# Layer 0's source sums: one burst of matmuls a quad, or four rounds spread over the next quad's blocks

## The reference

```python
def _L0_gnn_ref(x, edge_index, pos, gate_w1, gate_w2, msg_w1, msg_w2):
    row, col = (edge_index[0], edge_index[1])
    e = jnp.concatenate([x[row], x[col]], axis=-1)                        # 206250 x 128
    g1 = _lrelu(jnp.einsum('ef,hgf->heg', e, gate_w1))                    # 4 heads x 64
    alpha = _lrelu(jnp.einsum('heg,hog->heo', g1, gate_w2))               # 4 heads x 1
    a = pos[col][None, :, None] * jnp.exp(alpha)
    seg = lambda t: jax.ops.segment_sum(t, row, num_segments=N_NODES)
    rowsum = jax.vmap(seg)(a)
    inv = 1.0 / rowsum + 1e-16
    alpha_n = a * inv[:, row]
    m1 = _lrelu(jnp.einsum('ef,hgf->heg', e, msg_w1))                     # 4 heads x 128
    beta = _lrelu(jnp.einsum('heg,hog->heo', m1, msg_w2))                 # 4 heads x 64
    out_h = jax.vmap(seg)(alpha_n * beta)
    return jnp.mean(out_h, axis=0)
```

## Time and profile before

| | |
|---|---|
| median of 3 runs | 6655.64 us (6654.76 to 6658.46) |
| the profiled execution's own time | 6656.1 us, its span 6654.2 us |
| TensorE matmul, busy | 4382.8 us, 66% |
| VectorE, busy | 4799.1 us, 72% |
| GpSimd, busy | 3779.0 us, 57% |
| ScalarE, busy | 2634.2 us, 40% |
| layer 0's loop over blocks, about 700 to 4200 us | TensorE busy in 930.6 of 1000 us, VectorE in 836.3, ScalarE in 688.9 |
| TensorE's granted clock in that stretch | 1.00 of 2.4 GHz |

### The profile page before, as it was taken

How to read it: one execution, slowest core, us unless ns; L and a number is a source line. 1 busy time by engine, 2 the same in 40 slices (tenths; PEclk the granted TensorE clock), 3 DMA queues, 4 the chain that set the end, 5 groups by cost and what they waited for, 6 DMA issues and landing times.

```text
span 6654.2 us, 117791 instructions
## 1 busy us (share of the span) xinstructions
PE 4382.8 (66%) x24069; PEld 2598.3 (39%) x24069; DVE 4799.1 (72%) x10127; ACT 2634.2 (40%) x6054; POOL 3779.0 (57%) x3799
## 2 busy tenths in 40 slices
PE   3611999999999999999999999233333333333334
PEld 1211444444444444444444444133333333333333
DVE  6986788888888888888888888755555555555554
ACT  1200666666666666666666666200000000000000
POOL 0100555555555555555555555177777777777774
PEclk9955999999999999999999999655555555555555
DMA  8301333333333333333333333222222222222222
GB/s 237 152 0 33 73 72 72 72 72 72 72 72 72 72 72 72 72 72 72 71 71 72 72 71 72 70 51 50 51 50 51 51 50 51 50 51 51 50 51 59
DMA packets 485530, 452.11 MB, mean 68 GB/s; under 512 B 281672, under 2 KB 372041, under 8 KB 483593
## 3 DMA queue, kind: packets, MB, share of 16 engines
q0 software_dynamic: 137360, 180.87, 16.9%
q1 hardware_dynamic: 321118, 246.02, 13.3%
q10 hardware_dynamic: 27008, 24.74, 1.5%
HBM read 363.66 MB, written 87.55 MB: 68 GB/s over the span
## 4 chain that ended last, share of the span: by engine, by line
PE 27%; DVE 26%; issue 20%; POOL 19%; DMA 3%; ACT 3%; POOLq 1%; DVEq 1%; SPq 0%; ACTq 0%
POOL ends L749 11%; POOL work L749 8%; PE ps_beta L1620 6%; DVE work L1158 6%; PE ps_beta L1628 5%; PE ps_hidden L1568 5%; DVE work L1287 5%; PE ps_hidden L1569 4%; DVE beta L1163 4%; DVE ends_hot L1147 3%; PE ps_sum L1639 3%; DVE terms L1179 2%; ACT scaled L813 2%; DVE parts L1179 2%; PE ps_T L1557 1%
## 5 line engine op out<-in xcount | busy, mean ns | idle before, releaser
L1767 PE MATMUL ps_beta<-work,equal 128*128 128x128 f32 x3232 | 834.1, 440 | 1548.5 <-DVE work L1492 1548.5
L652 POOL DMA_INDIRECT ends<-split_table,src_sb x808 | 775.7, 960 | 1456.0 <-issue 1429.7
L1767 PEld LDWEIGHTS ps_beta<-work,equal 128*128 128x128 f32 x3232 | 719.4, 328 | 1663.4 <-issue 1523.3
L1158 DVE TENSOR_TENSOR work<-work,ps_hidden 128x512 f32<-128x512 f32 x1616 | 1099.7, 680 | 256.6 <-ACT work L813 256.0
L1568 PE MATMUL ps_hidden<-ends_parts,w_high 128*128 128x512 f32 x2424 | 1109.4, 458 | 1.2 <-ACT ends_hot L860 1.2
L813 ACT ACTIVATE work<-ps_hidden 128x512 f32<-128x512 f32 x1616 | 965.0, 597 | 325.1 <-DVE work L1158 316.0
L652 POOL DMA_INDIRECT ends<-split_table,gather_sb x808 | 805.5, 997 | 502.4 <-issue 374.6
L749 POOL DMA_INDIRECT work<-src_table,src_sb x808 | 814.8, 1008 | 336.6 <-issue 239.2
L749 POOL DMA_INDIRECT ends<-src_table,gather_sb x808 | 863.5, 1069 | 245.6 <-issue 245.3
L1620 PE MATMUL ps_beta<-work,msg_w_sb 128*64 128x512 f32 x3232 | 871.6, 617 | 192.8 <-DVE work L1158 192.8
L1569 PE MATMUL ps_hidden<-ends_hot,window 128*128 128x512 f32 x2424 | 958.9, 396 | 0.0
(11 more groups left out here) (156 smaller groups left out, 6189.6 us busy)
## 6 DMA issues: line engine op xcount, KB each, us to landing
window<-window_table SPq DMA_DIRECT2D x808, 96.2 KB
dst_rows_sb<-by_src SPq DMA_DIRECT2D x404, 128.0 KB
window_table<-parts SPq DMA_DIRECT2D x50, 770.0 KB, 3.3
ends<-in_edge_attr SPq DMA_DIRECT2D x202, 128.0 KB
key_rows<-in_edge_attr SPq DMA_DIRECT2D x202, 128.0 KB
sums<-key_rows POOLq DMA_DIRECT2D x404, 32.6 KB
sums<-parts ACTq DMA_DIRECT2D x10, 1305.0 KB, 14.9
ends<-split_table,src_sb POOLq DMA_INDIRECT x808
```

Of the source, the lines that this page charges most:

```text
L652: pool.indirect_dma_start(out=ends[m][:, t, :], out_offset=None, in_=split_table, in_offset=bass.IndirectOffsetOnAxis(ap=src_windows[m][:, ...
L1158: nc.vector.tensor_tensor(hidden[k][:, :], scaled[k % NL][:, :], ps_hidden[k % NL][:, :], ALU.max).then_inc(hidden_ready, 1)
L1767: last = nc.tensor.matmul(ps_beta[0][0:WIN, 0:W1], hot[m % 2][:, t, :].bitcast(F32), terms1_windows[m][:, t, :], start=(m == 0 and t == 0) ...
```

## The change

`sum_quad` becomes `sum_round`: one tile t of all four blocks, 4 of the 16 matmuls. Round t = m is issued in block m of the next quad, at the place where the whole burst stood in block 0. The sum of a quad is then complete at the end of block 3 of the next one, so the terms and one-hot matrices are doubled (the second sets lie in `parts0` and in `equal1`), VectorE waits for `summed` of one quad further back, `copy_quad` comes in block 0 instead of block 1 and one quad later, and the adds come one quad later. Because the buffers alternate by quad, TensorE's and VectorE's loops turn once in two quads (`quads`); ScalarE's and GpSimd's still turn once a quad (`fours_late`, whose first two quads are written out). VectorE sets the ones of the second set of terms ahead of its loop.

```diff
+        def quads(eng, body):
+
+            for quad in range(3):
+                for m in range(4):
+                    body(4 * quad + m, quad, m, quad % 2)
+            with eng.Fori(1, (NQ - 3) // 2) as i:
+                for odd in (1, 0):
+                    for m in range(4):
+                        body(8 * i + 8 - 4 * odd + m, 2 * i + 2 - odd, m, odd)
+            for quad in range(NQ - 2, NQ):
+                for m in range(4):
+                    body(4 * quad + m, quad, m, quad % 2)
...
# GpSimd
-                adds = m >= 2 and not first_four(b)
+                adds = m >= 2 and not first_two(quad)
...
                 if adds:
-                    add_rows(quad - 1, 2 * m - 4)
+                    add_rows(quad - 2, 2 * m - 4)
...
# ScalarE
                 scale_chunk(b, 2)
-                if m == 1 and not first_four(b):
-                    copy_quad(quad - 1)
+                if m == 0 and not first_two(quad):
+                    copy_quad(quad - 2)
                 scale_chunk(b, 3)
...
                 scale_pair(NB - 1, 1)
+                copy_quad(NQ - 2)
                 copy_quad(NQ - 1)
...
# VectorE
-            def spread_weights(b, quad, m):
+            def spread_weights(b, quad, m, odd):
 
                 dve.wait_ge(exp_ready, b + 1)
                 if m == 0:
-                    wait(dve, summed, quad)
+                    wait(dve, summed, quad - 1)
...
+                for m in range(4):
+                    nc.vector.memset(terms_quads[1][m][:, :, W0 - 1:W0], 1.0).then_inc(ones_set, 1)
...
# TensorE
-            def sum_quad(b, quad):
-
-                pe.wait_ge(terms_ready, 2 * b + 2)
-                pe.wait_ge(src_hot_ready, b + 1)
-                wait(pe, quad_copied, quad)
-                for t in range(T):
-                    for m in range(4):
-                        last = nc.tensor.matmul(ps_sum[m * WIN0:(m + 1) * WIN0, 0:W0], hot_quad[m][:, t, :].bitcast(F32),
-                                                terms_quad[m][:, t, :], start=(t == 0), stop=(t == T - 1))
-                last.then_inc(summed, 1)
+            def sum_round(b, quad, t, odd):
+
+                if t == 0:
+                    pe.wait_ge(terms_ready, 2 * b + 2)
+                    pe.wait_ge(src_hot_ready, b + 1)
+                    wait(pe, quad_copied, quad)
+                for m in range(4):
+                    last = nc.tensor.matmul(ps_sum[m * WIN0:(m + 1) * WIN0, 0:W0], hot_quads[odd][m][:, t, :].bitcast(F32),
+                                            terms_quads[odd][m][:, t, :], start=(t == 0), stop=(t == T - 1))
+                if t == T - 1:
+                    last.then_inc(summed, 1)
...
                 pair_product(b, 1)
-                if m == 0 and begun:
-                    sum_quad(b - 1, quad - 1)
+                if not first_four(b):
+                    sum_round(b - 1 - m, quad - 1, m, 1 - odd)
```

More of the change, by code:

```diff
@@ L70 @@
 assert P * RUN >= EP and RUN == 4 * B and NP <= 1 << FIELD
-assert COPIES == 2 and NT % CH == 0 and NB >= 12 and ROWS * W0 % (P * 5) == 0
+assert NQ % 2 == 1 and COPIES == 2 and NT % CH == 0 and NB >= 12 and ROWS * W0 % (P * 5) == 0
 def gnn(nc, x, src, dst, src_rows, dst_rows, dst_all, edge_attr, edge_weight, node_vec, node_vec1, node_vec1_n2,
@@ L315, in gnn @@
         quad_copied = sem("quad_copied")
+        ones_set = sem("ones_set")
         gates_done = sem("gates_done")
@@ L348, in fours, with fours_late, first_two @@
                 body(NB - 4 + m, NB // 4 - 1, m)
+        def quads(eng, body):
[9 more added lines that the diff above has]
+                    body(4 * quad + m, quad, m, quad % 2)
+        def fours_late(eng, body):
+            for b in range(8):
+                body(b, b // 4, b % 4)
+            with eng.Fori(2, NQ - 1) as i:
+                for m in range(4):
+                    body(4 * i + m, i, m)
+            for m in range(4):
+                body(NB - 4 + m, NQ - 1, m)
         def early(b):
             return isinstance(b, int) and b < 2
+        def first_two(quad):
+            return isinstance(quad, int) and quad < 2
         def first_four(b):
@@ L677, in edges0_windows @@
                 if adds:
-                    add_rows(quad - 1, 2 * m - 3)
+                    add_rows(quad - 2, 2 * m - 3)
             pool.wait_ge(tail_step, 2)
@@ L693, in _ @@
                 pool.wait_ge(zeroed, 16 * 5 * COPIES)
-                fours(pool, edges0_windows)
-                for m in range(4):
-                    add_rows(NQ - 1, m)
+                fours_late(pool, edges0_windows)
+                for quad in range(NQ - 2, NQ):
+                    for m in range(4):
+                        add_rows(quad, m)
                 pool.wait_ge(quad_added, 64 * NQ)
@@ L1179, in weigh_pair, with match_src, edges0_windows @@
                 nc.vector.tensor_tensor(
-                    terms_quad[m][:, :, a * 2 * D:(a + 1) * 2 * D].rearrange("p t (h d) -> p t h d", d=D),
+                    terms_quads[odd][m][:, :, a * 2 * D:(a + 1) * 2 * D].rearrange("p t (h d) -> p t h d", d=D),
                     ps_beta[a][:, :].rearrange("p (t h d) -> p t h d", t=T, d=D),
-                    terms_quad[m][:, :, H * D + 2 * a:H * D + 2 * a + 2].unsqueeze(3).broadcast_to([P, T, 2, D]),
+                    terms_quads[odd][m][:, :, H * D + 2 * a:H * D + 2 * a + 2].unsqueeze(3).broadcast_to([P, T, 2, D]),
                     ALU.mult).then_inc(terms_ready, 1)
-            def match_src(b, quad, m):
+            def match_src(b, quad, m, odd):
                 if m == 0:
-                    wait(dve, summed, quad)
-                nc.vector.tensor_tensor(hot_quad[m], columns[:, 0:WIN0].unsqueeze(1).broadcast_to([P, T, WIN0]),
+                    wait(dve, summed, quad - 1)
+                nc.vector.tensor_tensor(hot_quads[odd][m], columns[:, 0:WIN0].unsqueeze(1).broadcast_to([P, T, WIN0]),
                                         src_offset[:, bass.ds(b * T, T)].unsqueeze(2).broadcast_to([P, T, WIN0]),
                                         ALU.is_equal).then_inc(src_hot_ready, 1)
-            def edges0_windows(b, quad, m):
+            def edges0_windows(b, quad, m, odd):
                 half, j = 2 * quad + m // 2, m % 2
@@ L1196, in edges0_windows @@
                 before_quad, before_m = quad - (m == 0), (m + 3) % 4
+                before_odd = 1 - odd if m == 0 else odd
                 if begun:
@@ L1378, in _ @@
             with dve.If(fit):
+                dve.wait_ge(row_out[0], 16 * ((NT + 1) // 2))
+                dve.wait_ge(row_out[1], 16 * (NT // 2))
+                dve.wait_ge(tables_split, 32)
+                for m in range(4):
+                    nc.vector.memset(terms_quads[1][m][:, :, W0 - 1:W0], 1.0).then_inc(ones_set, 1)
                 match_near(0, 0, 0)
@@ L1381, in _ @@
                 rectify_chunk_windows(0, 1)
-                fours(dve, edges0_windows)
+                quads(dve, edges0_windows)
                 rectify_pair(NB - 1, 1)
-                spread_weights(NB - 1, NQ - 1, 3)
-                match_src(NB - 1, NQ - 1, 3)
-                weigh_pair(NB - 1, 0, 3)
-                weigh_pair(NB - 1, 1, 3)
+                spread_weights(NB - 1, NQ - 1, 3, 0)
+                match_src(NB - 1, NQ - 1, 3, 0)
+                weigh_pair(NB - 1, 0, 3, 0)
+                weigh_pair(NB - 1, 1, 3, 0)
             with dve.Else():
@@ L1735, in _ @@
                 first_product_windows(0, 1, 0, 0)
-                fours(pe, edges0_windows)
+                pe.wait_ge(ones_set, 4)
+                quads(pe, edges0_windows)
                 turn_pair(NB - 1, 1)
-                sum_quad(NB - 1, NQ - 1)
+                for t in range(T):
+                    sum_round(NB - 1, NQ - 1, t, 0)
             with pe.Else():
```

27 lines of the change are left out of this document (13 added, 14 removed).

## The result

The changed kernel takes 6746.26 us (median of 4 runs, 6741.89 to 6748.13), the kernel before 6655.9 in 4. The ratio is 1.0134, with a 95% interval from 1.0117 to 1.0152: 90 us slower. The prediction said 6741. The profiled execution took 6748.13 us, its span is 6746.5.

What follows compares the result with a forecast made beforehand. A ring of waits over TensorE, ScalarE and VectorE, with no engine full, was taken to set the time. The terms 38 - 8 + 46 + 9 = +85 us on 6656.1 gave 6741 us, range 6688 to 6806.

Steps and rivals of the forecast that it cites:

- A: Layer 0's loop, behind `pair_product(b, 1)`: four rounds cost 2.28 us a quad against 1.90 for one burst, +38 us.
- C: Moved `copy_quad` in block 0: waits 1.20 us for the last add, 0.47 a copy reaches the ring, +46 us.
- B: Block after the loop's turn: the round gives ScalarE's branch slack, saving 0.08 us a quad, -8 us.
- D: End of layer 0: two sums left uncopied, their copies and adds one behind the other, +9 us (6 to 10).
- ring of waits: Layer 0's blocks: waits through TensorE, ScalarE and VectorE set the 8.19 us, without slack where the sums stand.
- covered copy: Rival at the moved copy: the add lands early enough or ScalarE has more room, 6695 us; chance 0.12.
- fetched loop: Rival: VectorE's longer loop must fetch instructions at its turns, +62 us, 6803; chance 0.11.
- faster rival: Rounds fall into TensorE's idle time, mostly before `pair_product(b, 0)`, saving 1.90 us a quad, 6475 us; chance 0.10.

## Why the prediction was right

The places, the mechanism of A and C and the total were right; B's mechanism was not, and part of the agreement is luck. The two profiled spans lie 6746.5 - 6654.2 = 92.3 us apart. By stretches that is: up to the first sum pass -4.5 (714.0 to 709.5), the stretch of the sums +81.3, the end +6.8, and the second layer +8.7, which is what is left over.

| term | predicted | measured |
|---|---|---|
| A, four rounds for one | +38 | +38.8 (four rounds against one burst, both with the late copy) |
| B, the turn of the loop | -8 | -1.8 (burst with the late copy against before) |
| C, the moved copy | +46 | +44.3 (with the early against the late copy) |
| D, the end of layer 0 | +9 | +6.8 |
| not predicted | | -4.5 and +8.7 |
| sum | +85 | +92.3 |

The measured A, B and C are steps from the kernel before to the changed one by way of two variants, so they add up to the +81.3 by construction; the sum is no further test of them. What tests them one by one are the lengths of single blocks and, for C, the run with the burst and the early copy and the one with two buffers.

- **What bounds the kernel.** The ring of waits through TensorE, ScalarE and VectorE was read rightly: what stands between `pair_product(b, 1)` and the next first product is paid in full (8.19 to 8.77, 8.33 to 8.90), and what stands some 3 us later in the same ring, in front of `pair_product(b, 0)`, is free (8.19 stays 8.19).
- **A** held to 0.01 us a quad (0.39 against 0.38). The Trainium skill's rule on a change of tiling mode ("TensorEngine Tiling (Array Packing)", Key Properties) agrees in its direction with the rows behind `pair_product(b, 1)`: 0.11 to 0.16 us for every cut more. In the idle place the round's neighbour ahead of it is `gate_product`, with 32 columns too; by the rule one change fewer is due there. The rows show no shorter round: `pair_product` starts 0.62 us behind the round's first pass, where the first product came 0.58 behind it. Its whole length lies in time that was idle. What a cut costs was thus measured, and whether the mode makes it was not told apart.
- **B** had the wrong mechanism. The prediction let the round give 0.57 us of slack to ScalarE's branch of the ring and so save 0.08 at each turn, and put nothing for TensorE and VectorE turning half as often. With the late copy the block behind a turn goes from 8.43 to 9.02 us where TensorE and VectorE turn too, as they did in each quad before: 0.59 more, the round's whole length and no slack. It goes to 8.93 where they do not turn. With the burst in place of the rounds the two are 8.44 and 8.39. So what is saved is saved at the turns that the two engines no longer make, 0.05 to 0.09 us each. Over the loop B is -1.8 us without the rounds and about -3 with them (8.97 on average against 8.43 + 0.57), not -8. The error is 5 to 6 us.
- **C** came out in its steps, with two errors that nearly cancel. The last add lands 2.5 us after its start (2.45 predicted). The copy usually waits 1.06 us (1.20), VectorE idles 0.46 in the block shown (0.4 to 0.5), and 0.36 us a copy reaches the block (0.47). That makes 35 us. The six rare long waits, which the prediction did not have, add about 8.5; the stretch shows 44.3 in all, 0.45 a copy. Two of these six are lengthened by a lower granted clock. The two experiments that take the wait away, one by the copy's place and one by a second buffer, give 43 and 44 us back.
- **D** is 2 us under the +9, within its bounds of 6 to 10.
- **Rivals.** The covered copy (6695) is off: there is a wait. The fetched loop (6803) is off: 34 and 22 packets in the whole kernel. The faster rival gave 6475 for rounds that fall into TensorE's idle time. The changed kernel does not do that, since its rounds stand at the other place; the kernel that puts them there takes 6478.

By the medians the change costs 90.4 us; the four measured terms make 88.1. That they come within 3 us of the predicted 85 is in part luck: B is 6.2 us dearer than predicted, and C and D are 1.7 and 2.2 cheaper. C alone is met by luck too, as said. The +8.7 and -4.5 are readings of single profiles, and the medians leave only 2.3 us for both.

## What to carry to other kernels

Where a ring of waits over several engines sets the time, find its edges in the timeline before moving work: the same four rounds cost 2.3 us a quad at one place of the block and nothing some 3 us later in it. Cutting a burst pays as far as the pieces fall into gaps: one round at a time was free there and took 2.7% off the kernel, two at a time overran by 0.31 us each and still took 1.8% off, and at the first place each cut cost 0.11 to 0.16. When a copy is moved, look at what still reads its target. Here the last transfer that reads it lands 2.5 us after its start, the copy has to wait for that, and everything queued behind the copy waits with it. A second buffer and a later place in the queue both cure it. Look at the spread of such a wait and not only at its mean: six long ones of 98 made a fifth of the cost here.

## What the runs showed that I had not expected

- The usual wait of the early copy behaves as the fixed room of 0.73 us has it: 0.96 came through in the median, as expected. The 14 turns with longer waits make some 22 us over it, which against a base 6 us lower than expected is the 15 us above the expected total; in eight of the 14 TensorE's granted clock fell to 0.50 for 3.4 us or more. The kernel before and the variants with a late copy show neither in the loop.
- Chips differ more than the change: the same kernel before took 6656 to 6661 us on three occasions and 6841 and 6843 on another chip. There its loop over layer 0 is 1.2% longer (3543.2 against 3499.9 us) and the second layer's gathers 6% (2396.1 against 2258.9), at the same mean granted clock, 0.791. What makes that was not tried.
